# A graph network's first attention pass: the destinations' rows as three bf16 terms in place of f32

## The reference

```
edge_feat  = concat(h[src], h[dst])
messages   = relu(edge_feat @ msg_W1 + msg_b1) @ msg_W2 + msg_b2
att        = sigmoid(relu(edge_feat @ att_W1 + att_b1) @ att_W2 + att_b2)
aggregated = segment_sum(messages * att, dst)
h          = mlp(concat(h, aggregated)) + h + global_repr
```

## Time and profile before

| | us |
|---|---|
| median of 3 runs (6523.01 to 6523.32) | 6523.08 |
| the profiled execution | 6518.71 |
| its span, from first to last instruction | 6517.0 |
| TensorE busy in the span | 5097.5 (78%) |
| TensorE weight loads (beside matmuls) | 3386.5 (52%) |
| VectorE busy | 3210.5 (49%) |
| GpSimd busy | 2411.9 (37%) |
| ScalarE busy | 1691.7 (26%) |

### The profile page before, as it was taken

One profiled execution on the slowest core, in us unless ns is written; L12 is line 12 of the kernel. 1 busy time (PEld: TensorE's weight loads), 2 busy tenths in 40 slices (PEclk: granted clock), 3 DMA queues, 4 the chain that ended last, 5 costly groups with the idle time before them and its releaser, 6 DMA issues. The chain is left out here.

```text
span 6517.0 us, 95366 instructions
## 1 busy us (share of the span) xinstructions
PE 5097.5 (78%) x29088; PEld 3386.5 (52%) x29088; DVE 3210.5 (49%) x8514; ACT 1691.7 (26%) x4273; POOL 2411.9 (37%) x2524
## 2 busy tenths in 40 slices
PE   3555777999998878887998999999999987444443
PEld 1334555888875667776444444444444444333333
DVE  5887996888876777776653212111121123122221
ACT  3006995555543333333001011010010012000000
POOL 0780003666745777774000000000000002777776
PEclk7658998999998999998999999999999998555555
DMA  3457997555544444443854554544535524111112
GB/s 112 158 164 262 326 327 246 161 161 161 161 116 125 130 130 131 131 130 75 311 192 177 192 177 146 193 155 167 195 133 188 196 71 177 53 53 53 53 53 57
DMA packets 460315, 1009.70 MB, mean 155 GB/s; under 512 B 66081, under 2 KB 309718, under 8 KB 449494
## 3 DMA queue, kind: packets, MB, share of 16 engines
q1 hardware_dynamic: 348454, 711.13, 32.2%
q0 software_dynamic: 111536, 293.76, 15.9%
HBM read 768.42 MB, written 236.21 MB: 154 GB/s over the span
## 5 line engine op out<-in xcount | busy, mean ns | idle before, releaser
L1870 POOL DMA_INDIRECT ring<-rows,stage x1428 | 1369.4, 959 | 1116.3 <-ACT stage L1929 604.1
L1723 POOL DMA_INDIRECT ring<-rows,stage x808 | 764.3, 946 | 2711.5 <-ACT stage L1707 2465.6
L1366 PE MATMUL ps<-strip,trans_part 128*128 128x512 f16 (+1 forms) x8232 | 1606.0, 356 | 23.1 <-DVE trans_part L1283 23.1
L1366 PEld LDWEIGHTS ps<-strip,trans_part 128*128 128x128 bf16 x8232 | 755.5, 98 | 927.7 <-issue 76.9
L1955 PE MATMUL ps<-here,spread 128*128 x3264 | 955.0, 417 | 217.0 <-DVE ring L1904 180.8
L1775 PE MATMUL ps<-ring,mark 128*128 128x128 f32 x1616 | 414.4, 438 | 584.9 <-DMA ring<-rows,stage 583.6
L1904 DVE TENSOR_TENSOR ring<-ring,ps 128x512 f32<-128x512 f32 x816 | 561.0, 688 | 403.7 <-PE ps L1955 238.0
L1975 PE MATMUL ps<-ring,mark 128*128 128x128 f32 x3264 | 734.9, 313 | 3.4 <-issue 0.5
L1955 PEld LDWEIGHTS ps<-here,spread 128*128 128x128 f32 x3264 | 575.3, 196 | 310.8 <-issue 256.2
L1775 PEld LDWEIGHTS ps<-ring,mark 128*128 128x128 f32 x1616 | 357.1, 326 | 642.3 <-issue 642.3
L1275 DVE TENSOR_TENSOR trans<-ps,be 128x512 f32<-128x512 f32 x96 | 66.3, 691 | 1185.3 <-PE ps L1356 1185.3
(11 more groups left out here) (342 smaller groups left out, 5399.5 us busy)
## 6 DMA issues: line engine op xcount, KB each, us to landing
strip<-adj SPq DMA_DIRECT2D x392, 800.0 KB, 4.2
adj<-piece SPq DMA_DIRECT2D x120, 640.0 KB, 4.0
locs<-loc_rows SPq DMA_DIRECT2D x420, 128.0 KB, 3.1
ahead<-ahead_piece SPq DMA_DIRECT2D x125, 320.0 KB, 4.1
back<-back_piece SPq DMA_DIRECT2D x125, 320.0 KB, 4.5
sheet<-ahead SPq DMA_DIRECT2D x25, 1600.0 KB
sheet<-back SPq DMA_DIRECT2D x25, 1600.0 KB
ring<-rows,stage POOLq DMA_INDIRECT x2236, 2.5
```

The costliest lines, as they stand in the source:

```text
L1366: last = eng.matmul(k.ps[:, b, 0:cols], part[:, (step * NW + w) % TABLES, m, t * D:(t + 1) * D], strip[:, at % RING, c0:c0 + cols], start= ...
L1723: eng.indirect_dma_start(ring[:, t, :], None, rows, bass.IndirectOffsetOnAxis(stage[:, t:t + 1], 0)).then_inc(s_full[q], 16)
L1870: eng.indirect_dma_start(ring[:, t, :], None, rows, bass.IndirectOffsetOnAxis(stage[:, t:t + 1], 0)).then_inc(s_full[q], 16)
```

## The change

`first_rows` splits each destination row into three bf16 terms: the high term is the row rounded to bf16 (ScalarE), the middle one the rounded rest, the low one the rounded rest of that. VectorE makes the two subtractions, on whole groups of 128 x 1280, in a software pipeline over `GROUPS + 2` = 7 rounds. Buffers of destination rows and terms are three deep; the terms go to HBM laid out as they are read back, 4800 KB in place of 3200. The source rows' stores and the global mean stay. The mean's reduction lies in the round after the last group.

In the first attention pass `here` is a tile of three terms, `spread` is bf16, and every tile's expansion is three bf16 matmuls that accumulate in PSUM. In the second pass `parts` is 1: `spread` and `here` stay f32. The f32 table is now allocated inside step 1.

```diff
--- before.py
+++ after.py
@@ -22,6 +22,7 @@
 J = 36
 NTP = NT + J
 T4, T16 = 4, 16
+PARTS = 3
 BANK = 512
 NB = -(-NP // BANK)
 COL = NP
@@ -1806,7 +1807,8 @@
     W2 = 2 * D
     ring = k.sb("ring", [P, NQ * QUAD, W2], F32, own)
     mark = k.sb("mark", [P, NQ, QUAD, P], F32, own)
-    spread = k.sb("spread", [P, NQ, QUAD * P], F32, own)
+    parts = here.shape[1]
+    spread = k.sb("spread", [P, NQ, QUAD * P], F32 if parts == 1 else BF16, own)
     locs = k.sb("locs", [P, NQ, QUAD * P], BF16, own)
     stage = k.sb("stage", [P, NQ * QUAD], I32, own)
     lanes = k.sb("lanes", [P, P], BF16, own)
@@ -1952,8 +1954,9 @@
                 eng.wait_ge(s_add, g * 2 + (pair + 1))
                 for j in range(2):
                     t = pair * 2 + j
-                    last = eng.matmul(hid[:, j, :], spread[:, q, t * P:(t + 1) * P], here[:, bass.ds(cols[t] * 2, W2)],
-                                      start=True, stop=True)
+                    for m in range(parts):
+                        last = eng.matmul(hid[:, j, :], spread[:, q, t * P:(t + 1) * P], here[:, m, bass.ds(cols[t] * 2, W2)],
+                                          start=m == 0, stop=m == parts - 1)
                 last.then_inc(s_exp, 1)
 
             def body(i, last):
@@ -2054,18 +2057,22 @@
     nc = k.nc
     f = k.first
     glob = f.glob
-    G, HALF = 5, 2 * D
+    G, HALF, DEEP = 5, 2 * D, 3
+    GROUPS = NW // G
     k.rows0 = nc.dram_tensor("rows0", [NP, HALF], F32, kind="Internal").ap()
-    k.here0 = nc.dram_tensor("here0", [NP, HALF], F32, kind="Internal").ap()
+    k.here0 = nc.dram_tensor("here0", [P, PARTS, NW, HALF], BF16, kind="Internal").ap()
     k.h0 = nc.dram_tensor("h0", [P, NW * D], F32, kind="Internal").ap()
     k.early = nc.dram_tensor("early_rows", [EARLY * QUAD, P, HALF], F32, kind="Internal").ap()
     with ExitStack() as own:
         mean_wide = k.sb("mean_wide", [P, P], F32, own)
         mean = k.sb("mean", [P, 1], F32, own)
-        src_st, dst_st = (k.sb(n, [P, 2, G, HALF], F32, own) for n in ("src_rows", "dst_rows"))
-        names = ("s_dve", "s_mean", "s_g", "s_mm", "s_row", "s_keep", "s_h")
-        s_dve, s_mean, s_g, s_mm, s_src, s_dst, s_h = (k.sem(x) for x in names)
+        src_st = k.sb("src_rows", [P, 2, G, HALF], F32, own)
+        dst_st = k.sb("dst_rows", [P, DEEP, G, HALF], F32, own)
+        part_st = k.sb("dst_parts", [P, DEEP, PARTS, G, HALF], BF16, own)
+        names = ("s_dve", "s_mean", "s_g", "s_mm", "s_row", "s_keep", "s_h", "s_high", "s_rest", "s_mid", "s_part")
+        s_dve, s_mean, s_g, s_mm, s_src, s_dst, s_h, s_high, s_rest, s_mid, s_part = (k.sem(x) for x in names)
         s_st = [k.sem(f"s_st{j}") for j in range(2)]
+        s_kept = [k.sem(f"s_slot{j}") for j in range(DEEP)]
         MEAN = 7
         of = lambda rows, g: rows[g * G * P:(g + 1) * G * P, :].rearrange("(w p) d -> p w d", p=P)
         with nc.Block() as block:
@@ -2081,25 +2088,44 @@
 
             @block.scalar
             def _(eng):
-                for w in range(NW):
-                    g = w // G
-                    eng.wait_ge(s_mm, w + 1)
-                    if g >= 2:
-                        eng.wait_ge(s_st[g % 2], 32 * (g // 2))
-                    eng.activation(src_st[:, g % 2, w % G, :], k.ps[:, w % MEAN, 0:HALF], ACT.Copy).then_inc(s_src, 1)
+                for g in range(GROUPS + 2):
+                    if g < GROUPS:
+                        if g >= 2:
+                            eng.wait_ge(s_st[g % 2], 16 * (g // 2))
+                        for w in range(g * G, (g + 1) * G):
+                            eng.wait_ge(s_mm, w + 1)
+                            eng.activation(src_st[:, g % 2, w % G, :], k.ps[:, w % MEAN, 0:HALF], ACT.Copy).then_inc(s_src, 1)
+                    if 0 <= g - 2:
+                        eng.wait_ge(s_rest, g - 1)
+                        eng.activation(part_st[:, (g - 2) % DEEP, 1, :, :], dst_st[:, (g - 2) % DEEP, :, :], ACT.Copy).then_inc(s_mid, 1)
+                    if 0 <= g - 1 < GROUPS:
+                        eng.wait_ge(s_dst, g * G)
+                        if g - 1 >= DEEP:
+                            eng.wait_ge(s_kept[(g - 1) % DEEP], 16 * ((g - 1) // DEEP))
+                        eng.activation(part_st[:, (g - 1) % DEEP, 0, :, :], dst_st[:, (g - 1) % DEEP, :, :], ACT.Copy).then_inc(s_high, 1)
 
             @block.vector
             def _(eng):
-                for w in range(NW):
-                    g = w // G
-                    eng.wait_ge(s_src, w + 1)
-                    if g >= 2:
-                        eng.wait_ge(s_st[g % 2], 32 * (g // 2))
-                    eng.tensor_tensor(dst_st[:, g % 2, w % G, :], k.ps[:, w % MEAN, HALF:2 * HALF], f.bias1[:, :], ALU.add).then_inc(s_dst, 1)
                 c = Count(eng, s_dve)
-                c.step(eng.tensor_reduce(mean[:, :], k.hT[:, 0:N], AX.X, ALU.add))
-                c.step(eng.tensor_scalar(mean[:, :], mean[:, :], 1.0 / N, None, ALU.mult))
-                eng.tensor_scalar(mean_wide[:, :], k.ones[:, 0:P], mean[:, 0:1], None, ALU.mult).then_inc(s_mean, 1)
+                for g in range(GROUPS + 2):
+                    if g < GROUPS:
+                        for w in range(g * G, (g + 1) * G):
+                            eng.wait_ge(s_src, w + 1)
+                            if g >= DEEP:
+                                eng.wait_ge(s_part, g - DEEP + 1)
+                            eng.tensor_tensor(dst_st[:, g % DEEP, w % G, :], k.ps[:, w % MEAN, HALF:2 * HALF], f.bias1[:, :], ALU.add).then_inc(s_dst, 1)
+                    if g == GROUPS:
+                        c.step(eng.tensor_reduce(mean[:, :], k.hT[:, 0:N], AX.X, ALU.add))
+                        c.step(eng.tensor_scalar(mean[:, :], mean[:, :], 1.0 / N, None, ALU.mult))
+                        eng.tensor_scalar(mean_wide[:, :], k.ones[:, 0:P], mean[:, 0:1], None, ALU.mult).then_inc(s_mean, 1)
+                    if 0 <= g - 1 < GROUPS:
+                        whole = dst_st[:, (g - 1) % DEEP, :, :]
+                        eng.wait_ge(s_high, g)
+                        eng.tensor_tensor(whole, whole, part_st[:, (g - 1) % DEEP, 0, :, :], ALU.subtract).then_inc(s_rest, 1)
+                    if 0 <= g - 2:
+                        eng.wait_ge(s_mid, g - 1)
+                        eng.tensor_tensor(part_st[:, (g - 2) % DEEP, 2, :, :], dst_st[:, (g - 2) % DEEP, :, :],
+                                          part_st[:, (g - 2) % DEEP, 1, :, :], ALU.subtract).then_inc(s_part, 1)
                 c.step(k.gates1.add(eng))
                 c.step(k.gates2.add(eng))
                 eng.wait_ge(s_g, 1)
@@ -2109,13 +2135,17 @@
             @block.sync
             def _(eng):
                 eng.dma_start(k.h0, k.h[:, :, :].rearrange("p w d -> p (w d)")).then_inc(s_h, 16)
-                for g in range(NW // G):
-                    eng.wait_ge(s_src, (g + 1) * G)
-                    eng.dma_start(of(k.rows0, g), src_st[:, g % 2, :, :]).then_inc(s_st[g % 2], 16)
-                    eng.wait_ge(s_dst, (g + 1) * G)
-                    eng.dma_start(of(k.here0, g), dst_st[:, g % 2, :, :]).then_inc(s_st[g % 2], 16)
+                for g in range(GROUPS + 2):
+                    if g < GROUPS:
+                        eng.wait_ge(s_src, (g + 1) * G)
+                        eng.dma_start(of(k.rows0, g), src_st[:, g % 2, :, :]).then_inc(s_st[g % 2], 16)
+                    if g >= 2:
+                        eng.wait_ge(s_part, g - 1)
+                        eng.dma_start(k.here0[:, :, (g - 2) * G:(g - 1) * G, :], part_st[:, (g - 2) % DEEP, :, :, :]).then_inc(s_kept[(g - 2) % DEEP], 16)
                 for j in range(2):
-                    eng.wait_ge(s_st[j], 32 * len(range(j, NW // G, 2)))
+                    eng.wait_ge(s_st[j], 16 * len(range(j, GROUPS, 2)))
+                for j in range(DEEP):
+                    eng.wait_ge(s_kept[j], 16 * len(range(j, GROUPS, DEEP)))
                 eng.wait_ge(s_h, 16)
         k.end_phase()
 
@@ -2127,18 +2157,23 @@
     att_sum = f.att_sum
     own = ExitStack()
     with own:
-        here = k.sb("here", [P, NW, 2 * D], F32, own)
         rows = k.rows0
-        again = [(here[:, :, :], k.here0.rearrange("(w p) d -> p w d", p=P)),
-                 (k.h[:, :, :].rearrange("p w d -> p (w d)"), k.h0), (k.x[:, :, :], a["x"])]
         for step in range(2):
-            if step:
+            spot = own.enter_context(ExitStack())
+            if not step:
+                here = k.sb("here_parts", [P, PARTS, NW, 2 * D], BF16, spot)
+                again = [(here[:, :, :, :], k.here0), (k.h[:, :, :].rearrange("p w d -> p (w d)"), k.h0), (k.x[:, :, :], a["x"])]
+                wide = here.rearrange("p m w d -> p m (w d)")
+            else:
+                here = k.sb("here", [P, NW, 2 * D], F32, spot)
+                wide = here.rearrange("p (m w) d -> p m (w d)", m=1)
                 with ExitStack() as inner:
```

(3 more changed lines are left out.)

## The result

The changed kernel takes 6558.88 us (6553.8 to 6564.98, 4 runs) against 6523.2 (6523.01 to 6527.25, 4 runs): ratio 1.0051, 95% interval 1.0036 to 1.0066. It is **slower by half a per cent**, where 6472 was forecast. The profiled execution took 6564.98 us (span 6563.3, 46.3 more than before), 6.1 above the median. In it the 46.3 us lie as follows: 14.2 in first_rows (the next phase begins at 189.91, not 175.71), 1.9 in the adjacency, **22.4 in pass 1** (from the load of its table to the last scatter 887.6 us, not 865.2), 0.7 between the passes, 5.4 in pass 2, whose instructions are the same, and 1.7 in the rest. Pass 1 was to give 65 us back; it took 22 more.

The account below looks back on a forecast made before the run. Pass 1 was taken as bound by expansion and VectorE's add alternating, then by gathers: -63.4 (gathers) + 0 (start) - 1.8 (end of pass 1) + 14 (first_rows) = -51 us, so 6472 us; range 6450 to 6508.

Parts of the forecast that it names:

- The step that failed: Pass 1, half quad: TensorE's products and scatter take 1.66 us, below the half's 1.75 us.
- The compute side "could run at" 3.6 to 3.65: Pass 1: with bf16 products, the two halves' compute work sums to 3.6 to 3.65 us a quad.
- The gathers as the next bound: Pass 1: GpSimd's gathers, 1.262 us each, set 3.79 us a quad; -63.4 us.
- Products: Pass 1 expansion: six bf16 products take 0.82 to 0.87 us in place of 1.12 for four f32 records.
- rival B: Pass 1 expansion: weight loads are not hidden, +0.28 us a half, +114 us, total 6651 us; chance 0.05.
- Rival C: Pass 1: the clock falls to 0.94, 3.83 us a quad, net -43 us, total 6480 us; chance 0.12.
- Rival A: Pass 1: the compute side stays the bound at 3.9 us a quad, net -28 us, total 6495 us; chance 0.20.
- Start of pass 1: Larger table load +4 us against 3.6 us saved in six expansions: 0 us, between -3.6 and +3.8.
- first_rows: Building the three terms on VectorE and ScalarE costs +14 us, bounds +8 to +22.

Follow-up runs that it names:

- a_short: Changed kernel, complete, with one window number a tile in TensorE's table (read of 4 registers, not 8), read ahead of the second expansion: 6489.94 us, ratio 0.9950.
- ng_a_pair: Changed kernel without the gathers and early rows of pass 1, with one read of 16 registers for two quads: 4.85 us a quad in pass 1.
- ng_a_one: Changed kernel without the gathers and early rows of pass 1, with the high term's product only: 4.31 us a quad in pass 1.
- a_again: Changed kernel, unedited, run again on a second chip: 7265.66 us, ratio 1.0003 against the kernel before there (7259.06 us).

## Why the prediction was wrong

- **The step that failed** is "TensorE's own work is 0.66 for the products and 1.0 for the scatter, 1.66: below that". It counted what the array does and not what the sequencer must do ahead of it. I had the sign in hand: "the other half, with register work for the next quad, is 2.1 long", and took the 0.1 by which it stood out for its price. The read is 0.59 + 0.15 us; the f32 passes covered all but 0.1 of it. The change shortens the cover from 1.12 to 0.8 us and puts three times as many issues ahead of the read, and I costed both at nothing. The halves came out at 2.41 and 1.79, not 1.84 and 1.8.
- **The compute side "could run at" 3.6 to 3.65.** Without register work it runs at 3.39, so the sum over VectorE and the array was, if anything, cautious; the missing term is worth at least 0.84 us a quad, since VectorE binds at 3.39.
- **The gathers as the next bound** (3.79 a quad, -63.4 us) were not reached in the changed kernel: their heads still wait. a_short comes near them at 3.89, not 3.79, and gives 45.9 us of pass 1; a gather there takes 1.30 us, not 1.262.
- **Products**: six in 0.81 to 0.91 us, forecast 0.82 to 0.87: close. So **rival B** falls: the loads are hidden. The Trainium skill, "TensorE: Matmul & The Clock Gate", section on LDWEIGHTS, has a load take columns / 1.2, which is 107 ns for 128 columns as an estimate from it. The trace after has a median of 96 ns (95 to 291), somewhat less.
- **Rival C**, the clock: pass 1 held 1.00 at 82% busy. The rival falls for this kernel; of the variants, one was at 0.85 in pass 1 (ng_a_pair) and one at 0.50 throughout (ng_a_one). Why they differ is not shown.
- **Rival A**, the compute side stays the bound, had the outcome's kind and not its cause: its sign came true (heads of quads still wait), but it stood on VectorE's slack, at 3.9 a quad and 6495 us, where 4.22 and 6559 were measured.
- **Start of pass 1**: from the load of the table to the first gather behind quad 0 are 33.9 us (1070.93 to 1104.83) against 37.0 (1054.83 to 1091.82): -3.1, within the bounds (-3.6 to +3.8). The larger table cost 0.7 us: the first product comes 18.6 us behind the load, not 17.9.
- **first_rows**: +14 forecast, +14.2 measured. Its parts, in the timeline after:

```profile
167.58 1.48 DVE L2124 TENSOR_TENSOR dst_rows<-dst_rows,dst_parts 128x1280 f32<-128x1280 f32 x1
168.97 1.48 DVE L2127 TENSOR_TENSOR dst_parts<-dst_rows,dst_parts 128x1280 bf16<-128x1280 f32 x1
170.56 1.75 DVE L2116 TENSOR_TENSOR dst_rows<-ps,bias 128x256 f32<-128x256 f32 x5
172.23 1.48 DVE L2124 TENSOR_TENSOR dst_rows<-dst_rows,dst_parts 128x1280 f32<-128x1280 f32 x1
180.26 2.91 DVE L2127 TENSOR_TENSOR dst_parts<-dst_rows,dst_parts 128x1280 bf16<-128x1280 f32 x2
```

  Subtractions take 1.48 us (forecast 1.49); a steady group takes 4.65 (167.58 to 172.23), less than the 5.7 of the sum; the first one takes 5.45 (157.46 to 162.91). The last low term ends at 183.17, forecast 184.5, and the next phase begins 6.74 us behind it, forecast 4.5. These errors nearly cancel, so the close figure is in part luck.
- **The loss in numbers**: a quad took 0.127 us more (4.225 against 4.098), 26 us over 204 quads; less the 3.1 at the start that is about 23, and 22.4 was measured, where -65 stood; with first_rows as forecast, what is left of the 97 us between forecast (-51) and profile (+46.3) is 9.7 us in phases that the change does not touch. A range that ended at 6508 had no room for a compute side slower than before; only rival B lay there.

## What to carry to other kernels

When products get faster, look at what the engine's sequencer does beside them: register reads and address arithmetic do not shrink, and what they cost is hidden in the array's busy time as long as that is long. (What the number of issues costs by itself was not measured.) A half or round that stands out by 0.1 us because of register work is a sign that it is just covered, not that it is cheap. Before such a change, set the sequencer's sum for a round (reads, arithmetic, issues by their number) against the array's; where it comes near, shorten the read and fold factors into the address operation that is there anyway. And where the same kernel has another time in another set of runs, take the disputed part out of the transfers and time it alone.

## What was not expected of the hardware

- A read of registers from SBUF on TensorE costs by the register: 0.331 us for 4, 0.591 for 8, 1.104 for 16 (a_short, after, ng_a_pair), and the bounding of its values 0.095 and 0.150 us for 4 and 8.
- An address operation of a product is 46 ns, but with constant addresses in all six products of a half a quad fell by 0.76 us (4.23 to 3.47), more than their sum (12 x 46 ns = 0.55), and there VectorE, 94% busy, bound it.
- A kernel with less work on TensorE can be slower by its clock: with one product in place of three the granted clock was 0.50 from 1200 to 1700 (4.31 us a quad), with a longer gap in every second quad 0.85, where the changed kernel with 82% busy had 1.00. That these clocks follow from the edits was not tested by a second run.
- The kernel before took 7266.7, 7259.06 and 7186.08 us on three chips, and on a fourth 7245.86 at one time and 6522.87 at another. The rate in pass 1 is known for a_again, on the second chip: 121 GB/s instead of 156.
